# Spreading B and C from two 48-row halves of the partitions, both issued in the middle of a slot

## The reference

```
h_n(t) = exp(dt(t) * A_n) * h_n(t-1) + dt(t) * B_n(t) * u(t)
y(t)   = sum over n of h_n(t) * C_n(t)  + u(t) * D_skip
x      = x + (y * silu(z)) @ w_out
```

## Time and profile before

| what | value |
|---|---|
| runs shown | 1589.63, 1590.91, 1592.43 us |
| the profiled execution | 1590.84 us, of which the span of the trace is 1588.8 us |
| mean granted TensorE clock | 0.982 |
| busy over the span | PE 95%, DVE 86%, POOL 71%, ACT 65% |
| steps 0 and 1 | up to 134 us |
| steps 2 to 15 | 134 to 1186 us |
| drains and the rest of the block program | 1186 to about 1335 us |
| LSTM and output | about 1335 us to the end |

### The profile page before, as it was taken

One profiled execution on the slowest core, in us unless ns is written; L12 is line 12 of the kernel. 1 busy time (PEld: TensorE's weight loads), 2 busy tenths in 40 slices (PEclk: granted clock), 3 DMA queues, 4 the chain that ended last, 5 costly groups with the idle time before them and its releaser, 6 DMA issues. The chain is left out here.

```text
span 1588.8 us, 17874 instructions
## 1 busy us (share of the span) xinstructions
PE 1507.8 (95%) x4975; PEld 770.8 (49%) x4975; DVE 1368.8 (86%) x1623; ACT 1024.9 (65%) x2179; POOL 1123.5 (71%) x536
## 2 busy tenths in 40 slices
PE   8999999999999999999999999999997888999994
PEld 3444434444444444444444444444432335999993
DVE  7405999999999999999999999999999896667998
ACT  3254757666676767676758576666767656776772
POOL 0325989898989898989989898989898861001221
PEclk9999999999999999999999999999998899999997
DMA  9867767676776767666777766667642423000002
GB/s 367 330 247 266 259 228 252 246 249 247 252 249 239 265 231 260 243 238 238 255 259 246 255 245 247 251 243 255 245 171 63 158 72 119 0 0 1 0 0 106
DMA packets 64955, 321.64 MB, mean 202 GB/s; under 512 B 6988, under 2 KB 7040, under 8 KB 31989
## 3 DMA queue, kind: packets, MB, share of 16 engines
q1 hardware_dynamic: 54001, 301.43, 52.6%
q10 hardware_dynamic: 10884, 19.41, 3.8%
HBM read 308.49 MB, written 12.32 MB: 202 GB/s over the span
## 5 line engine op out<-in xcount | busy, mean ns | idle before, releaser
L605 PE MATMUL bank<-ring,xh 128*128 128x512 f32 x2048 | 956.9, 594 | 14.0 <-DVE xh L1197 8.2
L1313 DVE TENSOR_TENSOR_SCAN work<-bank,hstate,work 128x512 f32<-128x512 f32 x512 | 627.7, 1267 | 20.5 <-ACT bank L900 15.7
L605 PEld LDWEIGHTS bank<-ring,xh 128*128 128x128 f32 x2048 | 388.1, 190 | 465.7 <-issue 423.4
L1082 POOL TENSOR_TENSOR work<-work 128x1024 f32<-128x1024 f32 x210 | 495.4, 2359 | 85.5 <-DVE work L1262 77.1
L900 ACT ACTIVATE bank<-work,a_neg 128x512 f32<-128x512 f32 x512 | 344.6, 686 | 250.5 <-DVE work L1313 247.1
L1254 DVE TENSOR_TENSOR work<-work,bank 128x1024 f32<-128x1024 f32 x256 | 309.8, 1215 | 63.3 <-POOL work L1058 54.4
L1262 DVE TENSOR_TENSOR work<-work,bank 128x1024 f32<-128x1024 f32 x168 | 201.0, 1196 | 20.2 <-POOL work L1082 20.2
L499 PE MATMUL bank<-bc_parts,sel 96*128 96x512 bf16 x425 | 163.4, 385 | 20.2 <-DVE work L1254 19.3
L1158 POOL TENSOR_TENSOR work<-work 128x256 f32 x32 | 28.6, 894 | 215.5 <-ACT work L961 215.5
L494 PE MATMUL bank<-work,w_sb 128*128 128x512 f32 (+2 forms) x352 | 176.3, 598 | 1.3 <-DVE work L1243 0.7
L1027 POOL TENSOR_TENSOR work<-work 128x1024 f32<-128x1024 f32 x48 | 113.5, 2364 | 19.0 <-ACT work L783 18.9
(11 more groups left out here) (152 smaller groups left out, 1574.4 us busy)
## 6 DMA issues: line engine op xcount, KB each, us to landing
ring<-adj_t SPq DMA_DIRECT2D x256, 1024.0 KB, 5.4
xh<-c_scratch SPq DMA_DIRECT2D x31, 256.0 KB, 3.3
work<-c_scratch ACTq DMA_DIRECT2D x28, 256.0 KB, 5.6
c_two<-c_scratch ACTq DMA_DIRECT2D x28, 256.0 KB, 5.0
xh<-x_rows SPq DMA_DIRECT2D x16, 256.0 KB, 7.0
work<-x_t SPq DMA_DIRECT2D x16, 256.0 KB, 5.2
x_scratch<-work ACTq DMA_DIRECT2D x16, 256.0 KB, 3.6
work<-x_scratch SPq DMA_DIRECT2D x1, 4096.0 KB, 13.2
```

The lines of the kernel that those rows point to most:

```text
L605: last = nc.tensor.matmul(mixed[:, :], xn[:, j, :], a, start=(j == 0), stop=(j == BLK - 1))
L1082: nc.gpsimd.tensor_tensor(out=acc, in0=hc[0] if n == 1 else acc, in1=hc[n % 2], op=ALU.add).then_inc(y_added, 1)
L1313: nc.vector.tensor_tensor_scan(hb[s % 2][:, h, :], da[h], dbu[s % 2][:, h, :], hstate[:, HV * s + h:HV * s + h + 1], ALU.mult, ALU.add).th ...
```

## The change

Three things are altered together.

1. The layout. `w_xp` gets its columns as three copies of B, then `dt`, 8 zero columns, then three copies of C, so that B's parts stand in partitions 0 to 47 and C's in 64 to 111. `sel` becomes 128 x (16*128), and a spread contracts over 48 rows starting at 0 or 64.
2. The making of the parts. It now works on all 112 rows at a time. The parts that a row has already given are taken out by a scale of 0 or 1 for each partition (`past_high`, `past_mid`), the second remainder goes to `r1`, and one more copy on ScalarE at slot 14 writes all of `bc_parts`. TensorE waits for that copy.
3. The order. The C spread of state `s-1` moves from the start of slot `s` to its middle, right ahead of the B spread.

```diff
-XPW = 3 * BC + DR
+PART_ROWS = 3 * DS
+C_ROW = P // 2
+XPW = C_ROW + PART_ROWS
...
-        sel = sb("sel", [PARTS * BC, BC * P], BF)
+        sel = sb("sel", [P, DS * P], BF)
...
-        bc_parts = [sb(f"bc_parts{i}", [PARTS * BC, CH], BF) for i in range(2)]
-        bc_mid = sb("bc_mid", [PARTS * BC, CH], BF)
+        bc_parts = [sb(f"bc_parts{i}", [XPW, CH], BF) for i in range(2)]
+        bc_mid = sb("bc_mid", [XPW, CH], BF)
+        past_high = sb("past_high", [P, 1])
+        past_mid = sb("past_mid", [P, 1])
...
-                def spread(bank_, ready, row, n, rows=bc_parts[par]):
-
-                    nc.tensor.matmul(bank_[n % 2][:, :], sel[:, row * P:(row + 1) * P],
-                                     rows[:, :], start=True, stop=True).then_inc(ready, 1)
+                def spread(bank_, ready, base, row, n, rows=bc_parts[par]):
+
+                    nc.tensor.matmul(bank_[n % 2][:, :], sel[base:base + PART_ROWS, row * P:(row + 1) * P],
+                                     rows[base:base + PART_ROWS, :], start=True, stop=True).then_inc(ready, 1)
...
-                            pe.wait_ge(low_ready, k)
-                            pe.wait_ge(mid_ready, k)
+                            pe.wait_ge(parts_ready, k)
...
                 def mid_slot(s):
                     shared_steps(s, 0.5)
                     if not drains(k):
+                        if scan and s >= 1:
+                            spread_c(s - 1)
                         spread_b(s)
...
                 for s in range(16):
-                    if scan and not drains(k) and s >= 1:
-                        spread_c(s - 1)
...
-                        act.dma_start(c_dram[k - 1], dbc[DS:2 * DS, :]).then_inc(c_stored, 16)
-                        nc.scalar.activation(bc_parts[q][:, :], dbc[0:PARTS * BC, :], ACT.Copy).then_inc(high_ready, 1)
+                        act.dma_start(c_dram[k - 1], dbc[C_ROW:C_ROW + DS, :]).then_inc(c_stored, 16)
+                        nc.scalar.activation(bc_parts[q][:, :], dbc[0:XPW, :], ACT.Copy, scale=past_high[0:XPW, :]).then_inc(high_ready, 1)
...
-                        nc.scalar.activation(bc_mid[:, :], r1[0:PARTS * BC, :], ACT.Copy).then_inc(mid_rounded, 1)
-                        act.wait_ge(mid_rounded, k)
-                        nc.scalar.activation(bc_parts[q][BC:2 * BC, :], bc_mid[BC:2 * BC, :], ACT.Copy).then_inc(mid_ready, 1)
+                        nc.scalar.activation(bc_mid[:, :], r1[0:XPW, :], ACT.Copy, scale=past_mid[0:XPW, :]).then_inc(mid_ready, 1)
+                    if s == 14:
+                        act.wait_ge(r2_ready, k)
+                        nc.scalar.activation(bc_parts[q][:, :], r1[0:XPW, :], ACT.Copy).then_inc(parts_ready, 1)
...
-                        nc.gpsimd.tensor_tensor(out=bc_parts[q][2 * BC:3 * BC, :], in0=r1[2 * BC:3 * BC, :],
-                                                in1=bc_mid[2 * BC:3 * BC, :], op=ALU.subtract).then_inc(low_ready, 1)
-                        pool.wait_ge(low_ready, k)
+                        nc.gpsimd.tensor_tensor(out=r1[0:XPW, :], in0=r1[0:XPW, :], in1=bc_mid[:, :],
+                                                op=ALU.subtract).then_inc(r2_ready, 1)
+                        pool.wait_ge(r2_ready, k)
...
+            nc.vector.memset(past_high[:, :], 1.0).then_inc(past_set, 1)
+            nc.vector.memset(past_mid[:, :], 0.0).then_inc(past_set, 1)
+            dve.wait_ge(past_set, 2)
+            for base in (0, C_ROW):
+                nc.vector.memset(past_high[base:base + DS, :], 0.0)
+                nc.vector.memset(past_mid[base + 2 * DS:base + 4 * DS, :], 1.0)
```

More of the change, by code:

```diff
@@ L291, in build @@
         consts_in, bias_loaded = sems("consts_in bias_loaded")
-        consts_ready, sel_ready, init_done, fold_ready = sems("consts_ready sel_ready init_done fold_ready")
+        consts_ready, sel_ready, init_done, fold_ready, past_set = sems("consts_ready sel_ready init_done fold_ready past_set")
         folded, w_ih_ready, xl_one, xl_last, ones_stored = sems("folded w_ih_ready xl_one xl_last ones_stored")
@@ L310, in build @@
         halo_ready, tap_ready, tap_done, u_ready, sz_ready = sems("halo_ready tap_ready tap_done u_ready sz_ready")
[L311 removed]
+        high_ready, r1_ready, mid_ready, r2_ready, parts_ready = sems("high_ready r1_ready mid_ready r2_ready parts_ready")
         pos_dt, exp_dt, one_dt, log_dt = sems("pos_dt exp_dt one_dt log_dt")
@@ L510, in spread_c @@
                         pe.wait_ge(hc_done, hc_count(cs - 1, DS + n - 2, False))
-                    spread(c_bank, c_ready, DS + n, 0 if drains(k) else n)
+                    spread(c_bank, c_ready, C_ROW, n, 0 if drains(k) else n)
                 def spread_b(s):
@@ L516, in spread_b @@
                         wait(pe, dbu_done, DS * cs + (s + 1))
-                        spread(b_bank, b_ready, s + 2, s)
+                        spread(b_bank, b_ready, 0, s + 2, s)
                     if s >= DS - 2 and pre:
@@ L520, in spread_b @@
                         if k == 1 and n == 0:
-                            pe.wait_ge(sel_ready, 4)
+                            pe.wait_ge(sel_ready, 7)
                         if n == 0:
-                            pe.wait_ge(low_ready, k)
-                            pe.wait_ge(mid_ready, k)
+                            pe.wait_ge(parts_ready, k)
                         wait(pe, dbu_done, DS * (k - 1) + (n - 1))
-                        spread(b_bank, b_ready, n, n, bc_parts[1 - par])
+                        spread(b_bank, b_ready, 0, n, n, bc_parts[1 - par])
                 def mid_slot(s):
@@ L1011, in _ @@
             view = sel[:, :].rearrange("p (n m) -> p n m", m=P)
[L1012 to L1015, removed]
+            firsts = [base + DS * g for base in (0, C_ROW) for g in range(PARTS)]
+            for i, first in enumerate(firsts):
+                pool.wait_ge(sel_ready, i + 1)
+                nc.gpsimd.affine_select(out=view, in_=view, compare_op=ALU.not_equal, fill=1.0, base=-first,
+                                        pattern=[[-1, DS], [0, P]], channel_multiplier=1).then_inc(sel_ready, 1)
             pool.wait_ge(consts_in, 32)
@@ L1031, in pre_part @@
                         pool.wait_ge(high_ready, k)
-                        nc.gpsimd.tensor_tensor(out=r1[0:PARTS * BC, :], in0=dbc[0:PARTS * BC, :], in1=bc_parts[q][:, :],
+                        nc.gpsimd.tensor_tensor(out=r1[0:XPW, :], in0=dbc[0:XPW, :], in1=bc_parts[q][:, :],
                                                 op=ALU.subtract).then_inc(r1_ready, 1)
@@ L1041, in pre_part @@
                     if s == 13:
-                        pool.wait_ge(mid_rounded, k)
+                        pool.wait_ge(mid_ready, k)
                         if drains(k):
@@ L1465 @@
     w_xp = a[g + "w_xp"]
-    w_xp = np.concatenate([w_xp[:, DR:]] * PARTS + [w_xp[:, :DR]], axis=1)
+    b_cols, c_cols = w_xp[:, DR:DR + DS], w_xp[:, DR + DS:]
+    fill = np.zeros((DI, C_ROW - PART_ROWS - DR), np.float32)
+    w_xp = np.concatenate([b_cols] * PARTS + [w_xp[:, :DR], fill] + [c_cols] * PARTS, axis=1)
     w_dt = np.zeros((P, DI), np.float32)
-    w_dt[PARTS * BC:XPW] = a[g + "w_dt"]
+    w_dt[PART_ROWS:PART_ROWS + DR] = a[g + "w_dt"]
     weights = np.concatenate([a[g + "gcn_w"], a[g + "w_in"], by_half(w_xp), w_dt, by_half(a[g + "w_out"]),
```

## The result

The changed kernel takes 1626.09 us (median of four, 1625.59 to 1627.13) against 1591.58: a ratio of 1.0218, 95% interval 1.0206 to 1.023. The forecast was 1625. The profiled execution took 1627.13 us, with a span of 1625.3.

A forecast was written before the change was run, and what follows sets the result against it. PE's work was taken to set the step, with a loop of DVE and POOL nearly as long. 1590.9 + 33 (14 steps at +2.4 us) + 1 (drains) = 1625 us, range 1587 to 1665.

The forecast's parts named there:

- fewer rows buy nothing: PE matmuls: time goes by the 512 columns; a 104-row float32 matmul lasts 592 ns, as a 128-row one does.
- the halves overlap: Mid-slot spreads: any gain must come from a B and a C spread running in the array's two halves at once.
- The price of an excursion: Entering the small tile and returning to whole-array matmuls: 0.29 us beside the spreads, bounds 0.10 and 0.61; 17 a step.
- A pair: B and C spread sharing one stay in the small tile: 0.56 us instead of 0.44, +0.12 each, eleven a step.
- Less the 0.69 us that PE now waits for DVE, which a later PE no longer meets: PE's waiting at a step's first B spread would vanish, cutting +3.1 us of PE work to +2.4 a step.
- With PE slower this costs nothing: C spread some 2 us later: DVE's 0.4 us waits in some slots hidden by its slack; otherwise up to 6 us.
- The sum: Per step: pairs +1.3, lone spreads +1.7, less PE's 0.69 wait, +2.4; times 14 steps, +33 us.
- The drains and the rest: Some 30 lone B spreads in the drains: 9 us of PE work, 1 us on the path, bounds 0 and 9.
- The other edits: Slot 14 copy (0.63 us), scales (+0.16 of ACT a step), `sel`, memsets: hidden by idle time or margin, nothing added.
- Rival (a): Tiles change but the two spreads run one after the other: 4.2 us a step, 1650 us; part of outcomes given 0.77.
- (b): Changing tile costs nothing, spreads overlap, DVE becomes the bound: 1.0 us a step less, 1577 us; chance 0.14.
- (c): 48-row spreads use the whole array, no overlap or tile price: 1592, at most 1597; 0.09 shared with an unnoticeably cheap tile.

The follow-up runs named there:

- e5_lone_whole: Changed kernel, B spreads without a C beside them (slots 0, 2, 4, 9, 11 and drains) over 65 rows, whole array: 1614.36 us, ratio 1.0136.
- e6_same_half: Changed kernel, C spread of states other than GpSimd's reads rows 0 to 47 as the B spread does: 1645.11 us, ratio 1.0328.
- e9_tile_slot10: Changed kernel, C and B spreads ahead of the shared product in the middle of slot 10 alone: 1615.14 us, ratio 1.0153.
- e1_order: Kernel before, only the C spread moved to the middle of the slot, right ahead of the B spread; whole array: 1608.21 us, ratio 1.0092.
- the second profile: The changed kernel run once more, unaltered: 1624.05 us.
- e3_whole_start: e2_whole_mid with the C spread back at the start of the slot: 1593.85 us, ratio 1.0005.
- e4_tile_start: Changed kernel with the C spread back at the start of the slot, so B and C never run together: 1687.09 us, ratio 1.0588.
- e2_whole_mid: Changed kernel, each spread contracting over all 112 rows, so on the whole array: 1604.74 us, ratio 1.0071.
- e7_tile_first: Changed kernel, C and B spreads ahead of the shared product in the middle of slots 5, 6, 10, 11 and 12: 1621.66 us, ratio 1.0191.
- e10_order_slot10: e1_order with the spreads ahead of the shared product in the middle of slot 10 alone: 1594.77 us, ratio 1.0018.

## Why the prediction was right, and where it was not

**PE as the bound, fewer rows buy nothing, the halves overlap:** right. e5_lone_whole shows 65 rows at the old price, e6_same_half that the overlap comes from the halves.

**The price of an excursion:** forecast 0.29 us (0.10 in, 0.19 out), measured 0.30 (0.10 in, 0.20 out); the one place in the trace of before carried it. The Trainium skill's rule that a change of tiling mode drains TensorE (page "TensorEngine Tiling (Array Packing)", section "Key Properties") agrees with the late loads here, both ways (530.20 and 530.52, each with its matmul and not 0.43 us ahead). That page of the Trainium skill gives no price.

**A pair:** I put its second spread 0.05 us behind the first; the two stand in one line of 0.39 us, and a pair's 595.86 to 596.18 is as long as a single one's 598.10 to 598.42, so it is under 0.01. My reason for the 0.05, that the second load can only start behind the first, does not hold either: the two loads at 530.20 stand in one row of 0.10 us, where a single one (525.39) has 0.09. PE's work a step thus grew by 17 x 0.30 - 11 x 0.21 = 2.8 us, not 3.1.

**"Less the 0.69 us that PE now waits for DVE, which a later PE no longer meets":** this step failed, and in two ways that partly offset each other. PE's waits before were larger than the idle time that the profile gives, since a record's modelled end overlaps 0.16 us of the pause: by starts, the first B spread stood 0.86 us late (0.70 idle in the earlier trace rows and those 0.16), and with the DMA waits, counted in the same way, there were some 1.3 us a step. All of it is absorbed where nothing else intervenes: 2.8 - 1.3 = 1.5, the 1.4 of e9_tile_slot10. But in the changed kernel PE's wait for DVE stayed.

**"With PE slower this costs nothing", of the late C spread:** this is why. I compared DVE's busy time, 71.6 us, with the step and called the rest cover. The cover is not there where it is needed: the path from PE's first B spread over the C of state 9 and through DVE and POOL back to PE's next first B spread has none, as DVE's wait for POOL lies on it. I had looked at state 11 and priced at most 0.4 us a step; alone the order costs 15 us (e1_order), and in the changed kernel 0.6 us a step over e9_tile_slot10, 8 us in the steps and some 10 in all.

**The sum:** +33 us for the fourteen steps, against 26.3 in the thirteen counted here and 3.5 in the first, 29.8. The drains and the rest, 1 us forecast, came to 5.4 and in the second profile 3.2, within my 0 to 9; another 1.2 us lies in steps 0 and 1. So 1625 was met with a net price of the tile too large by some 13 us (2.4 against 1.4 a step), a price of the order too small by some 10, and a head and tail too small by 3 to 6. That these errors cancel to 1 us is luck.

**The other edits** (copy at slot 14, scales, `sel`, memsets): no cost that shows in the total of e3_whole_start. **Rival (a)** is refuted by the pair's one 0.39 us record, **(b)** by e4_tile_start, **(c)** by the loads. e2_whole_mid and e1_order are kernels of the kind that (c) describes, no excursion and a late C, and I gave that at most 1597 us: they took 1604.74 and 1608.21.

**Still open:** why the part after the start of step 16 is 3 to 5 us longer. 2.0 of them lie in the LSTM part, and 3.5 in one profile and 1.2 in the other ahead of it. No one edit goes with them: from that start to the end e3_whole_start (early C, whole array) took 406.8 us, e4_tile_start (early C, small tile) 402.6, e7_tile_first (late C, small tile) 403.1 and e10_order_slot10 (late C, whole array) 402.5.

## What to carry to other kernels

Packing two small matmuls into halves of the array pays only if enough of them share one stay in that tile: here a stay between whole-array float32 matmuls cost 0.30 us, and the pair in it saved 0.21. To price a moved instruction, don't compare an engine's busy time with the period; add up the loop that passes through its consumer from one step to the next, and see whether it closes in the period. A right total is no proof: it took one run with the order alone to show that a good part of the loss had another cause.

## What the hardware showed that I had not expected

The number of rows decides: 65 rows cost what 96 and more cost, 0.22 us, and 48 rows pay an excursion of 0.30. In a pair the second spread costs nothing that the trace resolves, and neither does its weight load: two loads stand in one row of 0.10 us. And a bf16 load that is not ahead costs 0.01 us, a float32 load 0.10, so an excursion costs more on its way back to the float32 matmuls, where the profile files a part under a line that was not changed. The mean of the adjacency record, 594 ns on the page of before, is 606 on that of after:

```profile
L608 PE MATMUL bank<-ring,xh 128*128 128x512 f32 x2048 | 959.9, 606 | 10.1 <-DVE xh L1208 8.2
```
